# Sharing the low halves of the expert weights differently between GpSimd and VectorE, with a new order of casts on ScalarE

## The reference

```python
y = _layernorm(patches, ln1_g, ln1_b)                  # 576 x 4096
y = jnp.einsum('bnd,dk->bnk', y, W_proj) + b_proj      # 4096 -> 192
h = _layernorm(y, ln2_g, ln2_b)
# attention: no projections; 12 heads of 8
q_vecs = jnp.cos(xs) * jnp.cos(theta)                  # xs: the first 96 of layernorm(h)
scores = jnp.einsum('bhsd,bhtd->bhst', q, q) / math.sqrt(D_K)
attn = jnp.einsum('bhst,bhtd->bhsd', jax.nn.softmax(scores), q)
h = h + attn @ W_combine.T
# mixture of 8 experts, the best 2 of each token
logits = xf @ router_w.T                               # xf = layernorm(h)
top_logits, top_idx = jax.lax.top_k(logits, 2); top_w = softmax(top_logits)
for e in range(8):
    w_e = jnp.sum(top_w * (top_idx == e), axis=-1)
    hid = silu(xf @ Wg[e].T) * (xf @ Wu[e].T)          # 192 -> 768
    out = out + hid @ Wd[e].T * w_e[:, None]
h = h + out
```

## Time and profile before

| | us |
|---|---|
| median of three runs | 261.39 |
| profiled execution | 259.68 |
| its span | 257.9 |
| TensorE matmul busy in the span | 201.1 (78%) |
| GpSimd busy | 149.1 (58%) |
| VectorE busy | 142.5 (55%) |
| ScalarE busy | 126.8 (49%) |

### The profile page before, as it was taken

How to read it: one execution, slowest core, us unless ns; L and a number is a source line. 1 busy time by engine, 2 the same in 40 slices (tenths; PEclk the granted TensorE clock), 3 DMA queues, 4 the chain that set the end, 5 groups by cost and what they waited for, 6 DMA issues and landing times.

```text
span 257.9 us, 4604 instructions
## 1 busy us (share of the span) xinstructions
PE 201.1 (78%) x1483; PEld 158.3 (61%) x1497; DVE 142.5 (55%) x409; ACT 126.8 (49%) x288; POOL 149.1 (58%) x195
## 2 busy tenths in 40 slices
PE   0599999899948778773399379987277999999970
PEld 0599999799936456553257155655145676767640
DVE  4999982797595026274034047767494455454530
ACT  0523582975793664286347065653343344444430
POOL 8696094599993301339648998989862122223322
PEclk9999999999965555555559959999989999999997
DMA  6999999951784221307610286544531112232122
GB/s 217 422 431 266 414 325 398 276 211 45 210 252 128 51 74 44 84 2 209 184 55 0 57 238 163 125 107 101 140 118 19 15 18 31 40 56 38 15 26 22
DMA packets 19088, 36.29 MB, mean 141 GB/s; under 512 B 3673, under 2 KB 9081, under 8 KB 18553
## 3 DMA queue, kind: packets, MB, share of 16 engines
q1 hardware_dynamic: 15689, 27.43, 34.3%
q0 software_dynamic: 2944, 2.76, 7.5%
q10 hardware_dynamic: 432, 5.80, 5.7%
HBM read 31.63 MB, written 4.36 MB: 140 GB/s over the span
## 4 chain that ended last, share of the span: by engine, by line
PE 31%; POOL 28%; DVE 12%; ACT 9%; DMA 9%; issue 8%; POOLq 1%; ACTq 0%; DVEq 0%
POOL experts L408 14%; DMA stage<-w_exp 8%; POOL experts L507 3%; PE ps L1404 3%; DVE ps L956 3%; PE ps L1250 3%; PE ps L1402 3%; POOL out L612 3%; PE ps L1407 3%; PE ps L1406 3%; PE ps L1414 3%; ACT experts L669 2%; ACT experts L700 2%; DVE experts L916 2%; PE ps L1428 2%
## 5 line engine op out<-in xcount | busy, mean ns | idle before, releaser
L408 POOL TENSOR_TENSOR experts<-stage,experts 128x528 bf16<-128x528 f32 x60 | 72.7, 1281 | 40.4 <-ACT experts L669 40.3
L1200 PE MATMUL ps<-experts 128*117 128x193 f32 (+1 forms) x320 | 56.4, 338 | 9.6 <-DVE experts L916 9.6
L1200 PEld LDWEIGHTS ps<-experts 128*117 128x117 f32 (+1 forms) x320 | 54.9, 188 | 9.9 <-issue 9.8
L1138 DVE TENSOR_TENSOR shared<-shared,ps 128x256 f32<-128x256 f32 x48 | 20.2, 420 | 62.8 <-ACT shared L817 62.8
L669 ACT CAST experts<-stage 128x528 f16<-128x528 f32 x64 | 38.5, 631 | 25.1 <-DMA stage<-w_exp 25.1
L817 ACT ACTIVATE shared<-ps 128x256 f32<-128x256 f32 x48 | 18.4, 384 | 32.6 <-PE ps L1407 32.5
L653 ACT ACTIVATE experts<-experts 128x468 f32<-128x468 f32 x40 | 22.8, 590 | 19.0 <-POOL experts L507 9.4
L1414 PE MATMUL ps<-ident,shared 128*128 128x128 f32 x96 | 19.6, 288 | 14.8 <-DVE shared L1138 14.7
L1414 PEld LDWEIGHTS ps<-ident,shared 128*128 128x128 f32 x96 | 13.1, 146 | 27.6 <-DVE shared L1138 19.9
L612 POOL DMA_INDIRECT out<-shared x8 | 12.4, 1550 | 29.7 <-ACT shared L842 27.0
L1428 PE MATMUL ps<-experts,shared 128*128 128x192 f16 (+1 forms) x96 | 24.0, 250 | 1.6 <-DVE shared L1143 1.6
(11 more groups left out here) (221 smaller groups left out, 357.0 us busy)
## 6 DMA issues: line engine op xcount, KB each, us to landing
stage<-w_exp SPq DMA_DIRECT2D x64, 264.0 KB, 3.1
experts<-x_t ACTq DMA_DIRECT2D x3, 1888.0 KB, 10.2
experts<-w_proj SPq DMA_DIRECT2D x4, 768.0 KB, 7.6
experts<-x_t SPq DMA_DIRECT2D x4, 472.0 KB, 8.2
experts<-x_t SPq DMA_DIRECT2D x1, 1888.0 KB, 14.7
slot_x<-experts SPq DMA_DIRECT2D x1, 1032.0 KB, 15.9
shared<-slot_x SPq DMA_DIRECT2D x8, 129.0 KB, 2.3
out<-h SPq DMA_DIRECT2D x1, 351.0 KB
```

Source lines behind the costliest of these rows:

```text
L408: ops.tensor_tensor(lo_w[:, to + EW:to + EW + PW], stage[:, n % STAGES, :], hi_w[:, to:to + PW], ALU.subtract).then_inc(split_pool if on_p ...
L1200: last = mm(dst, xbuf[:, t % 2, k, 0:m], gw[:, k, :], start=k == 0, stop=k == KT - 1)
```

## The change

The change moves work between engines and along their queues; no operation's size or kind changes. Nothing on TensorE moves except that its waits for whole experts now count splits of both engines.

- VectorE splits 16 pieces instead of 4: 32 to 35 in the attention, 44 to 51 in steps 0 to 11 of the expert loop, and 60 to 63 as before. GpSimd splits 48 instead of 60.
- GpSimd splits three pieces more ahead of the square adds of tile 3. Pieces 40 to 43 now come before the routing arithmetic, and the eight splits between that arithmetic and the first `add_out` are gone. The fill of `qp` with ones stands later among the first constants.
- ScalarE casts pieces between the squares of tiles 1 and 3, and two instead of one in most gaps of the attention. It is at piece 48 instead of 42 when the expert loop begins, and casts one piece a step from step 2 on. The second group's cosine stands ahead of `weighed_out(2)`.
- SP issues the output's base copy behind piece 49 instead of 45.

The diff, without the loops' unchanged lines:

```diff
-    VEC_PIECES = (60, 61, 62, 63)
+    VEC_PIECES = (32, 33, 34, 35, 44, 45, 46, 47, 48, 49, 50, 51, 60, 61, 62, 63)
...
-            load_pieces(2 * STAGES, 46)
+            load_pieces(2 * STAGES, 50)
...
-            load_pieces(46, NP * E)
+            load_pieces(50, NP * E)
...
-            g.memset(qp[:, :, :, :], 1.0)
             g.memset(cum[:, :, :], 0.0)
...
             link(g.tensor_copy(away[:, :], away_i[:, :]))
+            g.memset(qp[:, :, :, :], 1.0)
...
             square_adds(0)
-            rests(0, 10)
+            rests(0, 13)
             square_adds(3)
...
-            rests(10, 36)
+            rests(13, 40)
             low_parts(0)
-            rests(36, 38)
+            rests(40, 41)
             low_parts(1)
-            rests(38, 40)
+            rests(41, 44)
...
             pool.wait_ge(out_base, 32)
-            rests(40, 48)
             add_out(0)
-            rests(48, 50)
+            rests(52, 54)
             scatter_rows(0, 2)
             add_out(1)
-            rests(50, 52)
+            rests(54, 56)
             scatter_rows(2, 4)
             add_out(2)
-            rests(52, 54)
+            rests(56, 58)
             scatter_rows(4, 7)
+            rests(58, 60)
             add_out(3)
-            rests(54, 56)
             scatter_rows(7, 10)
-            rests(56, 60)
             add_out(4)
...
-            squares(1, 0, NG)
-            high_parts(0, 5)
+            for j in range(NG):
+                squares(1, j, j + 1)
+                if j >= 3:
+                    high_parts(j - 3, j - 2)
+            high_parts(5, 7)
...
-                if 2 <= j < 7:
-                    high_parts(3 + j, 4 + j)
+                if j in (3, 5, 7):
+                    high_parts(7 + j // 2 - 1, 7 + j // 2)
...
-            high_parts(10, 12)
+            high_parts(10, 13)
             squares(3, 0, 3)
             load_x(4)
             for j in range(3, NG):
                 squares(3, j, j + 1)
-                if j < 6:
-                    high_parts(9 + j, 10 + j)
-            high_parts(15, 16)
+                high_parts(10 + j, 11 + j)
             squares(4, 0, 3)
-            high_parts(16, 17)
+            high_parts(18, 20)
             cosine_of(0)
             squares(4, 3, NG)
-            high_parts(17, 24)
+            high_parts(20, 26)
             turned(0)
             turned(1)
             turned(2)
+            high_parts(26, 27)
             attend(0)
-            high_parts(24, 25)
+            high_parts(27, 29)
             weighed_out(0)
             attend(1)
-            high_parts(25, 26)
+            high_parts(29, 31)
             weighed_out(1)
             attend(2)
-            high_parts(26, 27)
+            cosine_of(1)
             weighed_out(2)
-            high_parts(27, 28)
-            cosine_of(1)
             turned(3)
...
             attend(3)
-            high_parts(28, 29)
+            high_parts(31, 33)
             weighed_out(3)
             attend(4)
-            high_parts(29, 30)
+            high_parts(33, 35)
             weighed_out(4)
-            high_parts(30, 31)
+            high_parts(35, 36)
...
             both_choices(0)
-            high_parts(31, 37)
+            high_parts(36, 42)
...
             both_choices(1)
-            high_parts(37, 40)
+            high_parts(42, 45)
             sc.wait_ge(gap_ready, 1)
             a.activation(gexp[0:TOK, :], gap[0:TOK, :], ACT.Exp).then_inc(gexp_ready, 1)
-            high_parts(40, 42)
+            high_parts(45, 48)
...
             rows_high(0)
-            high = 42
+            high = 48
             for n in range(NSTEP):
...
-                more = min(2 if r == 0 and c else 1, NP * E - high)
-                high_parts(high, high + more)
-                high += more
+                if n >= 2 and high < NP * E:
+                    high_parts(high, high + 1)
+                    high += 1
...
             weighed(2)
+            rests(32, 34)
             normed(0)
             weighed(3)
+            rests(34, 35)
             weighed(4)
+            rests(35, 36)
             normed(1)
...
+                if r != 1 and c < 4:
+                    rests(44 + 2 * c + r // 2, 45 + 2 * c + r // 2)
                 if c in (5, 6) and r != 1:
                     rests(60 + 2 * (c - 5) + r // 2, 61 + 2 * (c - 5) + r // 2)
```

## The result

The changed kernel takes **246.0 us** (median; 245.33 to 246.59), the kernel before 261.3 on the same chip: ratio 0.943, interval 0.937 to 0.949. 246 was forecast, in a range of 241 to 254. The profiled execution took 246.59 us, its span is 244.7.

A forecast was written before the change was run, and what follows sets the result against it. The order on GpSimd was taken to cause 22.9 us of waiting in the 74.68 us loop (floor 51.8). Start of loop +3.3 and loop -17.5 gave -14.2: 245.5 for the profiled execution, forecast 246, range 241 to 254.

The forecast's parts named there:

- T: Start of step 0 of the expert loop, said to come 3.3 us later (+1.7 to +5.1).
- (a): Up to the first attention tile: one more cast 0.5 and GpSimd's extra splits 0.7, together +1.2 us.
- (b): Attention: the second group's cosine moved ahead gains 1.5 us; with (a), the second half starts 0.3 earlier.
- (c): Attention: `normed(0)` on VectorE waits for piece 33's cast, making the transpose of tile 4's outputs 3.9 us later.
- Piece 63: Loop: still split at the end of step 20, right before step 21 needs it; TensorE waits, +1.6 us.
- Piece 58: Loop: loadable only after VectorE splits 51 in step 11, so ScalarE's cast in step 12 waits; +1.8 us (0 to 3.1).
- Meetings with GpSimd's splits: Loop: VectorE's picks and splits wait while GpSimd runs a pair of splits; two hits counted, +2.0 us (0 to 6).
- the prediction's own sign: The prediction called itself wrong in the loop if more than 7 us of waiting is left there.
- GpSimd's path: Loop: GpSimd's arithmetic, adds and scatters, then chunk 8's row load, done 53.8 us after step 0; covered by TensorE.
- the ring: Rival, chance 0.13: the loop's staging buffers stay the bound, about five loads come 1.5 us late; 252 us.
- the front: Rival, chance 0.15 with GpSimd alone setting step 24: the part before the loop costs nothing, T moves -1; 242 us.
- shut out: Rival, chance 0.06: VectorE's eight splits in steps 0 to 11 each lose 2.65 us to GpSimd's; 267 us, slower.

The follow-up runs named there:

- five edits: Changed kernel with `normed(0)` ahead of the early splits, `gap` ahead of splits 41 to 43, pieces 51 and 63 earlier, GpSimd's loop splits one by one: 237.33 us.
- row of eight: Changed kernel with pieces 44 to 51 on GpSimd again, split in a row between routing arithmetic and first `add_out`: 252.18 us, ratio 0.964.

## Why the prediction was right, point by point

**The time** was right (-13.06 at step 24 against -14.2). Two terms missed in opposite directions, T by 1.2 and the loop by 2.3, and one cause was credited with too much. That 246 was met to the tenth is luck: the sum itself gives 245.5 for the profiled execution, which took 246.59, and 261.39 - 14.2 = 247.2 for the median; 246 is neither.

- *(a), +1.2 said:* the Exp of tile 0 came 0.52 later, just the cast. `turned(0)` started at 73.11 as before, so the 0.7 for GpSimd's extra splits was nothing.
- *(b), shift of -0.3 said:* `turn_queries(3)` 1.27 earlier, since (a) was smaller and the cosine gave 1.8 for 1.5. Within its bounds.
- *(c), +3.9 said:* 106.58 to 109.32, +2.74. The working was right link by link (`normed(0)` to the transpose 6.57 for 6.7); only the shift of (b) was off. The experiment with `normed(0)` first shows that the wait is the cause.
- *T, +3.3 said:* +2.12. From the transpose to step 0 the changed kernel gained 0.62, said 0.56.
- *Piece 63, +1.6 said:* 1.60, to the row. *Piece 58, +1.8 said:* ScalarE waited 2.24; with that wait gone the steps around it got only 0.7 shorter.
- *Meetings with GpSimd's splits, +2.0 for two:* this term was mis-sized. Three long ones came. Steps 9 to 17, in which they cost time, took 24.77 us for the 19.23 of three chunks like steps 6 to 8 (6.41 each); without the 0.7 of piece 58 that leaves an estimated 4.8 for the three, where 2.0 stood for two. With all meetings and both late pieces gone the loop is 50.93, that is 8.57 less; taking piece 63 early gave 1.76 at its step, which leaves 6.8 where 3.8 stood: 5.5 in steps 9 to 17, and most of the rest in steps 0 to 2 (7.86 us for 6.77), which the floor of 51.8, 0.9 too high, counted as work. 59.5 is within the 53.4 to 62.6 said, but by the prediction's own sign it is wrong in the loop: more than 7 us of waiting are left, 59.5 - 51.8 = 7.7.
- *GpSimd's path, 53.8 after step 0 said:* its arithmetic took some 1.8 longer, for 2.0. The load of chunk 8's rows starts at 183.20 and needs 2.3, so 54.8. The rows were turned at 187.67, 2.2 after they came: covered, as said. It was the next thing late as well: where TensorE's part alone got shorter (five edits) or GpSimd got its splits back (row of eight), TensorE waited for those rows.
- *The rest, 54.63 said:* 54.45.

**The step that failed is the cause behind -17.5.** The prediction named the order on GpSimd, with eight splits in a row behind the routing arithmetic, as the source of the loop's 22.9 us of waiting, and let 17.5 of them end with that row; that four pieces more are split ahead of the loop it named too, but gave no share. But the row of eight, put back at pieces 44 to 51, costs TensorE nothing in sum up to step 22: its halt of 6.3 us over an undisturbed step is about as long as the meetings and waits that came in its place. The new order without any new split on VectorE is enough to shorten the loop up to step 22 from 70.7 to 56.2 us. What VectorE's eight splits bought beside that order is GpSimd's time: the load of chunk 8's rows starts 5.5 us earlier, and step 24 comes 5.5 us earlier. And its four early splits were a loss of 4.0. The right number stood on a mechanism that was half of it. One thing stays open: no run has the splits on VectorE with the old order, so how much they would have brought alone isn't known.

Of the rivals, the ring did not stay the bound (one wait of 2.2 us), and the front was not free (+2.12 at step 0). VectorE's splits were not shut out: all eight of pieces 44 to 51 took 0.67 to 0.76, and the one long split was that of piece 60.

On the lock the Trainium skill's page "SBUF — State Buffer", section "Who interferes with whom", says that a VectorE instruction with two SBUF inputs and a GpSimd instruction that reads SBUF contend for a shared pair of ports, which is an exclusive lock. The trace agrees in kind: each held operation ended 0.57 to 0.70 us after the end of a split of GpSimd. The prediction read the Trainium skill there as saying that one instruction is the most that is lost. In this the trace differs: behind a pair VectorE nearly always waited for both (157.85 + 3.15 = 161.00, the pair's end 160.31), though not always: in the two kernels with a row of eight on GpSimd one pick each ended between two splits. The term by one instruction, 0.8, would have been further off than the 2.0.

## What to carry to other kernels

Before moving work to another engine, ask who waits for what stands behind it there: the same four splits cost 4.0 us on the engine that others wait for and nothing on the one that waits. Where two engines hold each other up with the same kind of work, try giving all of it to one of them, and not half to each: here that took the loop from 59.5 to 50.9 us, late pieces included. And a gain's cause is known only when the parts have been undone one by one: here the order of work, which looked like a detail, was enough for 12 of 15 us.

## What the runs showed of the hardware

- **A long halt is paid twice.** Step 6 of the kernel before, with its first halt, and step 7 behind it, then steps 3 to 20 of the changed kernel (TensorE's busy time is the first column, its granted clock the one behind the five engines):

```profile
142.88:150.95 8.07, 2.69 (x16) 1.69 (x15) 1.10 (x5) 1.87 (x5) 7.79 (x12) 0.83 0.45 125
150.95:155.67 4.72, 4.50 (x34) 3.36 (x33) 2.69 (x5) 2.91 (x9) 4.54 (x5) 0.56 0.83 240
```

```profile
138.57:184.45 45.88, 40.41 (x356) 27.12 (x355) 34.68 (x72) 25.27 (x71) 37.83 (x53) 1.00 0.43 110
```

  After 8.07 us with 2.69 of work the granted clock of the next step is 0.56, near the lower level (1.2 of 2.4 GHz), and a matmul of 128x512 takes 0.63 instead of 0.38 us. The row of eight shows it again: 0.55 in the step behind the wait for chunk 8's rows, which takes 3.22 us instead of 1.79. The changed kernel's many short waits, 5.47 of 45.88 us, left it at 1.00.
- **A held operation can have started first.** By its record VectorE's split at 171.58 started 0.38 ahead of GpSimd's pair at 171.96 and still ended 0.58 behind it; a pick at 149.28 started 0.60 ahead. In all runs 14 picks and splits started 0.15 to 0.64 us ahead of a split of GpSimd, and all 14 were held. GpSimd had an indirect DMA on record each time; whether that plays a part no run shows.
- **GpSimd's scatters alone held no split up:** beside them VectorE's twelve splits stayed at 697 to 706 ns.
- **It works the other way too.** GpSimd's routing arithmetic, from its first L543 to the copies of L591, took 11.54 to 11.55 us in the three kernels where VectorE had no split in that time (one is the row of eight, 134.03 to 145.58), 13.31 beside four splits (changed kernel) and 14.79 beside eight (all of the loop's splits on VectorE, with one pick more).
